# A DLRM tower with two cross layers: products of three fields summed over d on TensorE, and weights of both layers combined on the chip

## The chip, the cores and the metric

One core of one Trainium2 chip runs the whole kernel. The metric is the device time of one execution, in microseconds (us).

## The reference

Each of 1024 samples has 32 categorical fields, each an index into a table of its own; the rows fetched are vectors of 32 numbers d. Two cross layers follow, then a small tower. Everything is fp32.

```python
e = stack([tbl_f[ids[:, f]] for f in range(32)], axis=1)     # b, 32 fields, 32 d
x = e
for W in (W0, W1):                                           # W0: 1024 x 128, W1: 4096 x 128
    z = einsum('bhd,bmd->bhmd', e, x).reshape(b, 32 * prev, 32)
    x = einsum('bpd,pj->bjd', z, W)
    res.append(x)
z = sum(concatenate(res, axis=1), axis=-1)                   # sum over d: 256 numbers a sample
h = relu(concatenate([z, dense_ctx], axis=1) @ W_top1 + b_top1)
h = relu(h @ W_top2 + b_top2)
y = h @ W_top3
```

x1[j, d] is a weighted sum of products of two fields, and only its sum over d is used as an output; the second layer multiplies x1 by every field once more. So the output of the second layer is a weighted sum, over triples of fields, of the products of three fields summed over d.

## The kernel before

The work goes in 8 tiles of 128 samples. A tile has 4 units of 32 samples, which are gathered from the tables by POOL (32 indirect DMAs a tile, L272, 128 rows each), and 8 chunks of 16 samples, which are 512 columns (16 samples by 32 d).

Gathered rows lie in `emb`. SP stores them in DRAM (`scratch`, L204 to L213) and loads every chunk back as `fac` (L215 to L235): four reads with other strides put field pairs side by side on 128 partitions, so that three vector multiplications (L409, L417, L418) and one small one (L424) form all pairs of fields for 512 columns. Three quarters of the first layer's products are then split: ACT rounds them into `zh` (L285), DVE subtracts that from the exact value into `zl` (L429), and PE multiplies the high part by the high and the low half of the weights and the low part by the high half. This takes nine passes of the faster format fp32r (L476, L477, L480), one for the leftover pairs (L482), and one exact fp32 matmul of two instructions (L473). Their sum is x1 of the chunk, in `XO`.

Then, per chunk: ACT copies x1 out; DVE sums it over d (L441); PE transposes it (L489, 4 instructions) and multiplies it by the block-diagonal `eblk` (L514, 4 fp32 matmuls of two instructions each), which gives the sums over d of x1 times each field; ACT copies those into `G` (L314 to L321). Once a tile, 32 fp32 matmuls (L523, x2_products) multiply `G` by W1, and the tower runs (L534, L535, L544, L552: 22 fp32 matmuls of 128 columns).

The order is written by hand: in PE's loop (L589 to L605) chunk i's x1, the transposes of chunk i-1 and the products of chunk i-2 follow each other, and at fixed chunks of the next tile stand x2_products, hidden1, hidden2 and result. The other engines have loops of the same lags, and semaphores tie them. The last tile's end is last_tile (L555 to L583).

Of the kernel before, what the change touches and what calls it, by code (L numbers as in the profile page):

```python
# [6 lines left out]
F32R = mybir.dt.float32r  # L7
# [3 lines left out]
AX = mybir.AxisListType  # L11
# [16 lines left out]

def dlrm_cin_tower(nc, dense_t, ids, bases, table, w_top1, w_dense, vec_in, w_top2, w0_pairs, w0_rest, w1, scratch, out):
# [5 lines left out]
    F, D, J = N_FIELDS, DIM, P  # L35
# [3 lines left out]
    BANK = 512  # L39
    CHUNKS = P * D // BANK  # L40
    TOTAL = TILES * CHUNKS
    PAIRS = TOTAL // 2
    COLS = P * D
    BC = BANK // D
    GU = BC // NQ
    UNITS = 4
    PER = CHUNKS // UNITS
    UG = P // NQ // UNITS
    WIDTH = UG // NQ
    URUN = UG * D  # L50
    KT1 = 2
    N1, N2 = H1 // P, H2 // P
    WHOLE = 1
    SPLIT = SHIFTS - WHOLE
    RING = 6
    ZB = 3
    RAMP = 8
    RING16 = 4

    ctx = ExitStack()  # L60
    with ctx:
# [8 lines left out]

        ident = sb("ident", [P, P])
# [3 lines left out]
        w0f = sb("w0f", [P, SHIFTS, J])  # L75
        w0h = sb("w0h", [P, SPLIT, J], F32R)
        w0l = sb("w0l", [P, SPLIT, J], F32R)
        w16m = sb("w16m", [3 * F, 2, J], F32R)
        w1s = sb("w1s", [P, F, J])
        wt1 = sb("wt1", [P, KT1, H1])  # L80
# [7 lines left out]
        eblk = sb("eblk", [P, P // NQ, NQ, F])  # L88
        fac = [sb(f"fac{i}", [P, SHIFTS, BANK]) for i in range(RING)]
        b16 = [sb(f"b16{i}", [F, 2, BANK]) for i in range(RING16)]  # L90
        z = [sb(f"z{i}", [P, WHOLE, BANK]) for i in range(ZB)]
        zh = [sb(f"zh{i}", [P, SPLIT, BANK], F32R) for i in range(2)]
        zl = [sb(f"zl{i}", [P, SPLIT, BANK], F32R) for i in range(2)]
        z16 = sb("z16", [F, BANK])
        z16p = [sb(f"z16p{i}", [3 * F, BANK], F32R) for i in range(2)]
        x1 = [sb(f"x1{i}", [P, BC, D]) for i in range(3)]
        x1t = [sb(f"x1t{i}", [P, GU, P]) for i in range(2)]
        G = sb("G", [P, F, P])
        zf = sb("zf", [P, KT1, B])
# [4 lines left out]
        XO = [ps(f"XO{i}", [P, BANK]) for i in range(2)]  # L104
        U0 = ps("U0", [P, BANK])
        U1 = ps("U1", [P, BANK])
        ZS = ps("ZS", [P, SPLIT, BANK])
        WA = ps("WA", [P, BANK])
        M = WA[:, :].rearrange("p (a b) -> p a b", b=P)
# [5 lines left out]
        w1_loaded = sem("w1_loaded")  # L115
        tower_loaded = sem("tower_loaded")
        prep = sem("prep")
        eblk_zero = sem("eblk_zero")
        tower_zero = sem("tower_zero")
        wt3_made = sem("wt3_made")  # L120
        rows_made = sem("rows_made")
        gathered = [[sem(f"gathered{i}{j}") for j in range(UNITS)] for i in range(2)]
        stored = [sem(f"stored{j}") for j in range(UNITS)]
        et_made = sem("et_made")
        eblk_made = sem("eblk_made")
        loaded = [sem(f"loaded{i}") for i in range(RING)]
# [532 lines left out]
```

## Time and profile before

| what | us |
|---|---|
| median of 3 runs | 464.38 |
| lowest, highest | 462.21, 464.61 |
| profiled execution, own time | 463.55 |
| its span, first to last instruction | 461.7 |
| PE busy (matmul) | 407.0 |
| DVE busy | 355.7 |
| POOL busy | 310.7 |
| ACT busy | 293.5 |

The profiled execution's own time is 1.85 us over its span. Busy times are unions of instruction records on one engine. A matmul record's end lies after the start of the next one, so the pace of PE is read from start to start, or from a run of many divided by their count. An fp32 matmul is two instructions, a transpose or an fp32r matmul is one.

### The profile page before, as it was taken

To read this page: it belongs to the slowest core of one execution; us is meant where nothing else is said; L and a number is where in the kernel's file an instruction comes from. 1 tells how busy PE (TensorE), PEld (TensorE's weight loads), DVE (VectorE), ACT (ScalarE), POOL (GpSimd) and SP (SyncE) were. 2 spreads that over 40 slices of the span, in tenths; PEclk is the share of its full clock that TensorE was granted. 3 is DMA by queue.
4 is the path that set the end of the run, shared out by engine and by line. 5 is a ranking of instruction groups with operands and counts; after the bars stand their busy time and mean duration, and the time that the engine had idled before them with its cause. 6 is when DMAs were issued, how large, how long until landed. Compare 5 with 4: busy or idle time off the path is not lost.

```text
span 461.7 us, 7268 instructions
## 1 busy us (share of the span) xinstructions
PE 407.0 (88%) x2464; PEld 330.3 (72%) x2464; DVE 355.7 (77%) x399; ACT 293.5 (64%) x512; POOL 310.7 (67%) x262
## 2 busy tenths in 40 slices
PE   0014788889999999999999999999999999999987
PEld 0002456569877788868888888788888988798887
DVE  6024798997699888976989968997899689978700
ACT  1011577674677757864788588876788478847841
POOL 6777777887788787878787878788787777000000
PEclk9999999999999999999999999999999999999999
DMA  7368899775887668999899789888777659992000
GB/s 277 100 144 211 210 222 219 231 211 140 181 244 221 198 186 213 176 207 223 204 211 219 184 201 243 213 217 215 223 228 210 182 144 220 214 267 60 1 1 0
DMA packets 56659, 86.25 MB, mean 187 GB/s; under 512 B 10696, under 2 KB 21136, under 8 KB 56496
## 3 DMA queue, kind: packets, MB, share of 16 engines
q1 hardware_dynamic: 48432, 81.59, 62.4%
q0 software_dynamic: 8192, 4.21, 10.4%
q8 instruction: 20, 0.33, 0.4%
q14 instruction: 15, 0.12, 0.1%
HBM read 79.47 MB, written 6.30 MB: 186 GB/s over the span
## 4 chain that ended last, share of the span: by engine, by line
PE 54%; POOL 30%; issue 9%; DMA 4%; DVE 2%; ACT 1%; SPq 1%; POOLq 0%; DVEq 0%
POOL emb L272 30%; PE WA L523 9%; PE U L514 7%; PE XO L473 7%; PE XO L480 6%; PE XO L477 6%; PE XO L476 6%; PE U L489 4%; PE WA L544 2%; PE WA L534 2%; PE XO L482 2%; DMA fac<-scratch 2%; DMA emb<-in_table,rows 1%; PE WA L535 1%; PE WA L499 1%
## 5 line engine op out<-in xcount | busy, mean ns | idle before, releaser
L272 POOL DMA_INDIRECT emb<-in_table,rows x256 | 310.0, 1211 | 80.2 <-issue 77.7
L429 DVE TENSOR_TENSOR zl<-ZS,zh 128x1536 fp32r<-128x1536 f32 x64 | 112.1, 1752 | 34.5 <-ACT zh L279 34.4
L279 ACT ACTIVATE zh<-ZS 128x1536 fp32r<-128x1536 f32 x64 | 93.1, 1455 | 67.2 <-issue 39.3
L476 PE MATMUL XO<-zh,w0h 128*128 128x512 f32 x192 | 98.9, 515 | 2.8 <-ACT zh L279 2.8
L473 PE MATMUL XO<-z,w0f 128*128 128x512 f32 x128 | 67.4, 609 | 31.1 <-DVE z L409 31.1
L418 DVE TENSOR_TENSOR ZS<-fac 128x1024 f32<-128x1024 f32 x64 | 78.1, 1220 | 0.0
L477 PE MATMUL XO<-zh,w0l 128*128 128x512 f32 x192 | 76.9, 401 | 0.0
L409 DVE TENSOR_TENSOR z<-fac 128x512 f32<-128x512 f32 x64 | 43.8, 685 | 42.3 <-DMA fac<-scratch 41.9
L480 PE MATMUL XO<-zl,w0h 128*128 128x512 f32 x192 | 57.4, 407 | 13.2 <-DVE zl L429 12.7
L514 PE MATMUL U<-eblk,x1t 128*128 128x128 f32 x504 | 67.2, 276 | 0.0
L279 ACT ACTIVATE G<-U 128x512 f32<-128x512 f32 x63 | 38.0, 603 | 43.2 <-PE WA L523 40.7
L514 PEld LDWEIGHTS U<-eblk,x1t 128*128 128x128 f32 x504 | 61.2, 192 | 0.3
L476 PEld LDWEIGHTS XO<-zh,w0h 128*128 128x128 f32 x192 | 36.9, 192 | 31.3 <-ACT zh L279 13.6
L523 PE MATMUL WA<-G,w1s 128*128 128x128 f32 x512 | 58.5, 275 | 0.0
L523 PEld LDWEIGHTS WA<-G,w1s 128*128 128x128 f32 x512 | 57.8, 192 | 0.0
L480 PEld LDWEIGHTS XO<-zl,w0h 128*128 128x128 f32 x192 | 35.2, 190 | 27.6 <-DVE zl L429 20.1
L279 ACT ACTIVATE eblk<-WA 32x256 f32<-32x256 f32 x128 | 48.0, 375 | 6.5 <-PE WA L499 2.8
L477 PEld LDWEIGHTS XO<-zh,w0l 128*128 128x128 f32 x192 | 36.9, 192 | 18.2 <-issue 12.2
L441 DVE TENSOR_REDUCE zf<-x 128x16 f32<-128x512 f32 x64 | 43.2, 677 | 5.8 <-ACT x L279 4.9
L417 DVE TENSOR_TENSOR ZS<-fac 128x512 f32<-128x512 f32 x64 | 44.1, 690 | 1.1
L489 PE MATMUL U<-ident,x 128*128 128x128 f32 x256 | 38.7, 273 | 5.1 <-ACT x1t L279 5.1
L473 PEld LDWEIGHTS XO<-z,w0f 128*128 128x128 f32 x128 | 20.0, 196 | 31.3 <-issue 31.1
(76 smaller groups left out, 380.7 us busy)
## 6 DMA issues: line engine op xcount, KB each, us to landing
fac<-scratch SPq DMA_DIRECT2D x256, 256.0 KB
emb<-in_table,rows POOLq DMA_INDIRECT x256
scratch<-emb SPq DMA_DIRECT2D x32, 128.0 KB
b<-scratch SPq DMA_DIRECT2D x64, 64.0 KB, 6.1
w1s<-in_W SPq DMA_DIRECT2D x1, 2048.0 KB, 8.4
scratch<-emb SPq DMA_DIRECT2D x32, 64.0 KB
wt<-in_W_top SPq DMA_DIRECT2D x2, 512.0 KB, 9.4
z<-in_W_pairs SPq DMA_DIRECT2D x2, 256.0 KB, 2.8
```

The costliest lines, as they stand in the source:

```text
L272: eng.indirect_dma_start(emb[par][:, g, :], None, table, bass.IndirectOffsetOnAxis(rows[:, k, g:g + 1], 0))\
L279: return eng.activation(dst, src, ACT.Copy)
L417: eng.tensor_tensor(ZS[:, 0, :], f[:, 0, :], f[:, 3, :], ALU.mult).then_inc(zs_first, 1)
L418: eng.tensor_tensor(ZS[:, 1:, :], equal, fac[s][:, 2:4, :], ALU.mult).then_inc(zs_done, 1)
L429: eng.tensor_tensor(zl[i % 2][:, :, :], ZS[:, :, :], zh[i % 2][:, :, :].bitcast(F32), ALU.subtract)\
L473: eng.matmul(o, w0f[:, t, :], zb[:, t, :], start=(t == 0), stop=False)
L476: eng.matmul(o, w0h[:, t, :], zh[b][:, t, :], start=(WHOLE == 0 and t == 0), stop=False)
L477: eng.matmul(o, w0l[:, t, :], zh[b][:, t, :], start=False, stop=False)
L480: eng.matmul(o, w0h[:, t, :], zl[b][:, t, :], start=False, stop=False)
L489: t = eng.transpose(U0[:, P * u:P * u + P], flat[:, P * u:P * u + P], ident[:, :])
L514: m = eng.matmul(g_bank(i)[:, P * u:P * u + P], x1t[i % 2][:, u, :], eblk[:, at, :, :].rearrange("p v h -> p (v h)"), start=True, stop=True)
L523: m = eng.matmul(WA[:, 0:P], w1s[:, h, :], G[:, h, :], start=(h == 0), stop=(h == F - 1))
```

## The change

DRAM scratch, the loads from it, the split into high and low parts and x1 itself are gone. What takes their place:

- **Products.** Gathered units are transposed on PE (`ET`: partition = sample and d, column = group and field; a group is 4 samples, a unit 8 groups). ACT copies `ET` into the block-diagonal `eblk` of 33 columns a sample (32 fields and one of ones; 4 copies of 32 partitions) and once plainly into `eT`. DVE multiplies `ET` (PSUM) by `eT` (SBUF) in 11 instructions a unit (products, in three parts): all unordered pairs of the first 16 fields, all of the last 16.
- **Triples.** One slot is three groups (the third slot of a unit has two). For each group PE multiplies the transposed pairs (128 columns for `TA`, 128 for `TB`, 32 for `T3`) by `eblk` (132 columns): each result is a product of three fields summed over d. There are 96 slots, 24 matmuls a unit.
- **Copies.** ACT copies `TA` and `TB` into `TS` in three pieces each (side_copy), DVE copies `T3` in five (rest_copy). The bank `T3` is single, `TA` and `TB` are double.
- **Combined weights.** Before the loop PE multiplies W1 by W0 plus its transposed pair (w0_w1: 32 times 272 and 256 columns). In the first tile DVE adds what belongs to the same triple (weights, 12 portions, 70 additions and 4 copies). In slots 12 to 18 PE transposes the 56 blocks and ACT copies them to `C`.
- **Both outputs.** A tile is then 56 matmuls of 128 columns for the second layer (second) and 7 for the first (first), and the tower as before. Tile 0's stand in slots 19 to 26, those of tiles 1 to 6 in the slots of the tile after, tile 7's at the end.

The number of gathers, their size, the tower and the outputs stay. The diff, cut:

```diff
-            def load(k, n):
-                i = CHUNKS * k + n
-                at = scratch.offset + k * ROWS * COLS + BANK * n
-                if n % PER == 0:
-                    eng.wait_ge(stored[n // PER], STORES * (k + 1))
-                wait(eng, zs_done, i - RING + 1)
-                for a in range(2):
-                    eng.dma_start(fac[i % RING][:, a, :],
-                                  bass.AP(scratch.tensor, at + (4 - 4 * a) * COLS, [[COLS, F], [0, 4], [1, BANK]]))\
-                       .then_inc(loaded[i % RING], 16)
...
-            def products_split(i):
-
-                s = i % RING
-                f = fac[s][:, :, :]
-                wait(eng, zl_done, i)
-                equal = bass.AP(f.tensor, f.offset + BANK, [list(f.ap[0]), [0, 2], [1, BANK]])
-                eng.tensor_tensor(ZS[:, 0, :], f[:, 0, :], f[:, 3, :], ALU.mult).then_inc(zs_first, 1)
-                eng.tensor_tensor(ZS[:, 1:, :], equal, fac[s][:, 2:4, :], ALU.mult).then_inc(zs_done, 1)
...
-            def products(i):
-                zb, b, o = z[i % ZB], i % 2, XO[i % 2][:, :]
-                wait(eng, x1_kept, i - 1)
-                eng.wait_ge(z_done, i + 1)
-                for t in range(WHOLE):
-                    eng.matmul(o, w0f[:, t, :], zb[:, t, :], start=(t == 0), stop=False)
-                eng.wait_ge(zh_done, i + 1)
-                for t in range(SPLIT):
-                    eng.matmul(o, w0h[:, t, :], zh[b][:, t, :], start=(WHOLE == 0 and t == 0), stop=False)
-                    eng.matmul(o, w0l[:, t, :], zh[b][:, t, :], start=False, stop=False)
-                eng.wait_ge(zl_done, i + 1)
-                for t in range(SPLIT):
-                    eng.matmul(o, w0h[:, t, :], zl[b][:, t, :], start=False, stop=False)
-                eng.wait_ge(z16l_done, i // 2 + 1)
-                eng.matmul(o, w16m[:, i % 2, :], z16p[i // 2 % 2][:, :], start=False, stop=True).then_inc(x1_made, 1)
-
...
+            def w0_w1(h):
+
+                if h % (F // W1P) == 0:
+                    eng.wait_ge(w1_loaded[h // (F // W1P)], 16)
+                wait(eng, rt_kept, h - 1)
+                eng.matmul(TA[h % 2][:, 0:RTC], w1s[:, h, :], sym[:, 0:RTC], start=True, stop=True).then_inc(rt_made, 1)
+                p, x = divmod(h, 2)
+                if x == 0:
+                    wait(eng, rx_kept, p - 1)
+                m = eng.matmul(TB[p % 2][:, RAB * x:RAB * x + RAB], w1s[:, h, :], sym[:, RTC:], start=True, stop=True)
+                if x == 1:
+                    m.then_inc(rx_made, 1)
...
+            def full_adds(X, second, part):
+
+
+                Y = 1 - X
+                f, c = across(X)
+                if part == 0:
+                    dst = rt(HALF * Y, P * X + 64, [[RTC, HALF], [SUB, SUB], [1, SUB]])
+                    src = rx(HALF * X + SUB, 0, [[c, HALF], [f, SUB], [RAB, SUB]]) if second else \
+                        rx(HALF * X, SUB * f, [[c, HALF], [RAB, SUB], [f, SUB]])
+                    add(dst, dst, src, second_added if second else first_added)
+                    return
...
+            def products(u, part):
+
+                both = 2 * GROUPS
+                pairs, rest = zT[u % 2][:, :, :], z3[u % 2][:, :, :]
+
+                def apart(s):
+                    some = [[HALF, both], [SUB, 2], [1, SUB - s]]
+                    eng.tensor_tensor(view(pairs, off(s), [[P, both], [32, 2], [1, SUB - s]]), field(0, some), copied(s, some),
+                                      ALU.mult).then_inc(z_made, 1)
+
+                if part == 0:
+                    eng.wait_ge(eblk_made, (NQ + 1) * (u + 1))
+                    wait(eng, t3_made, TRIOS * (u - 1))
+                    eng.tensor_tensor(view(pairs, 64, [[P, both], [SUB, SUB], [1, SUB]]),
+                                      field(0, [[HALF, both], [1, SUB], [0, SUB]]),
+                                      copied(SUB, [[HALF, both], [0, SUB], [1, SUB]]), ALU.mult).then_inc(z_made, 1)
+                if part == 1:
+                    for s in range(1, 5):
+                        apart(s)
+                if part == 2:
+                    for s in range(5, SUB):
+                        apart(s)
+                    some = [[HALF, both], [SUB, 2], [1, 4]]
+                    eng.tensor_tensor(view(pairs, PAIRS, [[P, both], [32, 2], [1, 4]]), field(0, some), copied(0, some),
+                                      ALU.mult).then_inc(z_made, 1)
+                    some = [[F, GROUPS], [SUB, 4], [1, 4]]
+                    eng.tensor_tensor(view(rest, 0, [[THIRD, GROUPS], [4, 4], [1, 4]]), field(4, some), copied(4, some),
+                                      ALU.mult).then_inc(z_made, 1)
+                    eng.tensor_copy(view(rest, MORE, [[THIRD, GROUPS], [1, HALF]]), field(0, [[F, GROUPS], [1, HALF]]))\
+                       .then_inc(z_made, 1)
+
+            def rest_copy(t):
...
+                for q in range(NQ):
+                    eng.tensor_copy(view(ts[32 * q:32 * q + 32, :, :], P * REST + b0, [[4 * P, 2], [P, 4], [1, n]]),
+                                    view(T3[0:32, :], q, [[HALF + 1, 2], [4, 4], [C33, n]])).then_inc(t3_kept, 1)
+                eng.tensor_copy(ts[0:32, REST1, b0:b0 + n], view(T3[0:32, :], ONES, [[C33, n]])).then_inc(t3_kept, 1)
...
+            def side_copy(X, t, made, kept):
...
+                copy(view(ts[:, :, :], P * FULL[X] + b0, [[P, HALF + 1], [1, n]]),
+                     view(bank[:, :], full, [[1, HALF + 1], [C33, n]])).then_inc(kept, 1)
+                for e in range(2):
+                    at = (HALF + 1 if X else 0) + SUB * e
+                    copy(view(ts[64 * e:64 * e + 64, :, :], P * OWNS[X] + b0, [[P, SUB], [1, n]]),
+                         view(bank[0:64, :], at, [[1, SUB], [C33, n]])).then_inc(kept, 1)
+
+            def c_copy(q):
...
+            def triples(t):
...
+                    eng.wait_ge(rt_kept, F)
+                    eng.wait_ge(rx_kept, F // 2)
+                wait(eng, ta_kept, 3 * (t - 1))
+                pairs, rest = zT[u % 2], z3[u % 2]
+                for bank, z, cols, made in ((TA[t % 2], pairs, slice(0, P), ta_made), (TB[t % 2], pairs, slice(P, 2 * P), tb_made),
+                                            (T3[0:THIRD, :], rest, slice(0, THIRD), t3_made)):
+                    if made is tb_made:
+                        wait(eng, tb_kept, 3 * (t - 1))
+                    if made is t3_made:
+                        wait(eng, t3_kept, 5 * t)
+                    for x, g in enumerate(trio(r)):
+                        at = NQ * C33 * x
+                        m = eng.matmul(bank[:, at:at + NQ * C33], z[:, g, cols],
+                                       eblk[u % 2][:, g, :, :].rearrange("p v c -> p (v c)"), start=True, stop=True)
+                    m.then_inc(made, 1)
+
+            def second(k, pieces):
+                if pieces[0] == 0:
+                    eng.wait_ge(ta_kept, 3 * SLOTS_TILE * (k + 1))
+                    eng.wait_ge(tb_kept, 3 * SLOTS_TILE * (k + 1))
+                    eng.wait_ge(t3_kept, 5 * SLOTS_TILE * (k + 1))
+                    eng.wait_ge(c_kept, CB)
+                    wait(eng, y2_kept, k)
+                for kt in pieces:
+                    m = eng.matmul(WA[:, 0:P], C[:, kt, :], TS[k % 2][:, slot_of(kt), :], start=(kt == 0), stop=(kt == KT - 1))
+                if pieces[-1] == KT - 1:
+                    m.then_inc(y2_made, 1)
...
+        def y2_range(t):
+
+
+            k, j = divmod(t, SLOTS_TILE)
+            if k == 1:
+                return (0, range(14 * (j - 7), 14 * (j - 7) + 14)) if 7 <= j < 11 else None
+            if k > 1 and j < KT // Y2_PER:
+                return k - 1, range(Y2_PER * j, Y2_PER * j + Y2_PER)
+            return None
```

A chunk of 16 samples on PE before, with the waits on semaphores in brackets (`XO` is x1, `U` the banks of the transposes and of the products, `ZS` holds the products to be split):

```order
L473 MATMUL XO<-z,w0f 128x512 [waits z_done,x1_kept]
L476 MATMUL XO<-zh,w0h 128x512 [waits zh_done]
L477 MATMUL XO<-zh,w0l 128x512
L476 MATMUL XO<-zh,w0h 128x512
L477 MATMUL XO<-zh,w0l 128x512
L476 MATMUL XO<-zh,w0h 128x512
L477 MATMUL XO<-zh,w0l 128x512
L480 MATMUL XO<-zl,w0h 128x512 [waits zl_done]
L480 MATMUL XO<-zl,w0h 128x512 x2
L482 MATMUL XO<-z16p,w16m 128x512 [waits z16l_done]
L489 MATMUL U<-ident,x 128x128 [waits xt_kept,x1_kept]
L489 MATMUL U<-ident,x 128x128 x3
L514 MATMUL U<-eblk,x1t 128x128 [waits eblk_made,g_kept,xt_kept]
L514 MATMUL U<-eblk,x1t 128x128 x3
```

One unit of 32 samples in the steady part of the change on PE, which begins with the transposes of the unit after it (`T` is `T3`, `RX` holds the combined weights):

```order
L640 MATMUL ET<-ident,emb 128x128 [waits z_made,gathered03]
L640 MATMUL ET<-ident,emb 128x128
L661 MATMUL TA<-eblk,zT 128x132 [waits ta_kept,z_made]
L661 MATMUL TA<-eblk,zT 128x132 x2
L661 MATMUL TB<-eblk,zT 128x132 [waits tb_kept]
L661 MATMUL TB<-eblk,zT 128x132 x2
L661 MATMUL T<-eblk,z 32x132 [waits t3_kept]
L661 MATMUL T<-eblk,z 32x132 x2
L673 MATMUL WA<-TS,RX 128x128 x7
L661 MATMUL TA<-eblk,zT 128x132 [waits ta_kept]
L661 MATMUL TA<-eblk,zT 128x132 x2
L661 MATMUL TB<-eblk,zT 128x132 [waits tb_kept]
```

The first matmul of a unit waits for z_made, the eleven products of that unit, which DVE makes while PE works at the unit before it. Every `T` group waits for t3_kept, DVE's copies of the slot before.

DVE in the first tile of the change, from the first product of unit 1 on:

```order
L534 TENSOR_TENSOR zT<-ET,eT 128x16x64 [waits eblk_made]
L564 COPY TS<-T 32x8x12 [waits t3_made]
L564 COPY TS<-T 32x8x12 x3
L566 COPY TS<-T 32x12
L401 TENSOR_TENSOR RT<-RT,RX 128x16x64 [waits rx_kept,rt_kept]
L528 TENSOR_TENSOR zT<-ET,eT 128x16x2x7
L528 TENSOR_TENSOR zT<-ET,eT 128x16x2x6
L528 TENSOR_TENSOR zT<-ET,eT 128x16x2x5
L528 TENSOR_TENSOR zT<-ET,eT 128x16x2x4
L564 COPY TS<-T 32x8x12 [waits t3_made]
L564 COPY TS<-T 32x8x12 x3
L566 COPY TS<-T 32x12
```

Between the copies of `T` and the next products stands an addition to the weights. In later tiles the rows of L401 are missing, and the others come in the same order. Of before, one chunk on DVE:

```order
L435 TENSOR_TENSOR z16p<-z,z16p 32x512 [waits z16h_done]
L417 TENSOR_TENSOR ZS<-fac 128x512 [waits zl_done]
L418 TENSOR_TENSOR ZS<-fac 128x1024
L441 TENSOR_REDUCE zf<-x 128x2x8 [waits x1_kept]
L409 TENSOR_TENSOR z<-fac 128x512 [waits x1_made,loaded4]
L429 TENSOR_TENSOR zl<-ZS,zh 128x1536 [waits x1_made,zh_done]
```

The six rows became, for a unit, eleven products and fifteen copies of at most 1024 columns, tied to PE at both ends.

## Rows read from the trace of the kernel before

**Rows 1.** The page: engines, granted clock in 40 slices, chain by engine

```profile
PE 407.0 (88%) x2464; PEld 330.3 (72%) x2464; DVE 355.7 (77%) x399; ACT 293.5 (64%) x512; POOL 310.7 (67%) x262
...
PEclk9999999999999999999999999999999999999999
...
PE 54%; POOL 30%; issue 9%; DMA 4%; DVE 2%; ACT 1%; SPq 1%; POOLq 0%; DVEq 0%
```

**Rows 2.** Windows: busy us (instructions) of PE, PEld, DVE, ACT, POOL; clock, DMA, GB/s

```profile
31.00:41.00 10.00, 4.97 (x8) 2.32 (x8) 2.58 (x4) 2.59 (x3) 7.56 (x9) 1.00 0.62 161
51.00:61.00 10.00, 7.02 (x32) 4.31 (x31) 6.70 (x8) 7.37 (x12) 7.87 (x8) 1.00 0.90 232
200.00:440.00 240.00, 238.68 (x1494) 199.31 (x1493) 207.71 (x231) 173.92 (x305) 153.89 (x125) 1.00 0.77 192
```

**Rows 3.** Chain in order of time: start us, us, what, instructions

```profile
357.99 7.15 PE WA L523 x64
...
392.88 0.86 PE XO L473 x2
396.49 0.89 PE U L514 x8
...
407.26 7.15 PE WA L523 x64
```

**Rows 4.** Timeline of PE, 43 to 50 us: start us, us, instruction

```profile
43.20 1.65 PE L480 MATMUL XO<-zl,w0h 128*128 128x512 f32 x3 [5.88 <-DVE zl L429]
...
48.22 0.63 PE L476 MATMUL XO<-zh,w0h 128*128 128x512 f32 x1
48.65 0.58 PE L477 MATMUL XO<-zh,w0l 128*128 128x512 f32 x1
49.06 0.40 PE L476 MATMUL XO<-zh,w0h 128*128 128x512 f32 x1
49.29 0.39 PE L477 MATMUL XO<-zh,w0l 128*128 128x512 f32 x1
```

**Rows 5.** Timeline of DVE and POOL, 385.5 to 389.5 us

```profile
385.41 1.76 DVE L429 TENSOR_TENSOR zl<-ZS,zh 128x1536 fp32r<-128x1536 f32 x1 [0.25 <-ACT zh L279]
...
386.28 0.94 POOL L272 DMA_INDIRECT emb<-in_table,rows  x1 [0.30 <-issue]
...
387.20 0.70 DVE L417 TENSOR_TENSOR ZS<-fac 128x512 f32<-128x512 f32 x1
...
387.81 1.23 DVE L418 TENSOR_TENSOR ZS<-fac 128x1024 f32<-128x1024 f32 x1
...
388.95 0.67 DVE L424 TENSOR_TENSOR z<-b 32x512 f32<-32x512 f32 x1
389.01 1.43 POOL L272 DMA_INDIRECT emb<-in_table,rows  x1 [0.30 <-issue]
```

**Rows 6.** Groups: busy us, mean ns of one, idle before and releasers

```profile
L473 PE MATMUL XO<-z,w0f 128*128 128x512 f32 x128 | 67.4, 609 | 31.1 <-DVE z L409 31.1
...
L279 ACT ACTIVATE eblk<-WA 32x256 f32<-32x256 f32 x128 | 48.0, 375 | 6.5 <-PE WA L499 2.8
...
L489 PE MATMUL U<-ident,x 128*128 128x128 f32 x256 | 38.7, 273 | 5.1 <-ACT x1t L279 5.1
L279 ACT ACTIVATE x1t<-U 128x512 f32<-128x512 f32 x64 | 38.2, 598 | 0.3 <-PE U L489 0.3
...
L279 ACT ACTIVATE G<-U 128x512 f32<-128x512 f32 x63 | 38.0, 603 | 43.2 <-PE WA L523 40.7 <-PE U L514 2.3
...
L279 ACT ACTIVATE zf<-WA 128x128 f32<-128x128 f32 x8 | 2.2, 273 | 8.3 <-PE WA L523 8.3
...
L461 DVE TENSOR_SCALAR h<-XO,vec 128x128 f32<-128x128 f32 x2 | 0.7, 351 | 13.0 <-PE XO L570 13.0
```

**Rows 7.** Timeline of DVE, the first 10 us

```profile
6.40 3.47 DVE L390 MEMSET eblk<- 128x4096 f32 x1 [0.80 <-issue]
```

**Rows 8.** Timeline, the end of the span

```profile
455.56 0.28 ACT L279 ACTIVATE zf<-WA 128x128 f32<-128x128 f32 x1 [8.34 <-PE WA L523]
```

More of the change, by code:

```diff
@@ new lines, in own_adds @@
+            def own_adds(e, second):
+                f, c = (SUB, 1) if e == 0 else (1, SUB)
+                for s in range(1, SUB) if second else range(0, SUB):
+                    n = SUB - s if s else 4
+                    col = 32 * e + (off(s) if s else PAIRS)
+                    dst = own(0, 1 - e, col, [[XO, 2], [P, SUB], [1, n]])
+                    one = dst if second else rt(SUB * (1 - e), col, [[XS, 2], [RTC, SUB], [1, n]])
+                    h, other = (s, 0) if second else (0, s)
+                    two = rt(SUB * e + h, 64 + f * other, [[XS, 2], [c, SUB], [RTC + f, n]])
+                    add(dst, one, two, second_added if second else first_added)
@@ new lines, in _ @@
+            eng.wait_ge(w0_loaded, 16 * 2)
+            eng.tensor_tensor(sym[:, :], sym[:, :], raw, ALU.add).then_inc(sym_made, 1)
+            eng.wait_ge(zeroed, 5)
+            for i in range(2):
+                for v in range(NQ):
+                    eng.memset(eblk[i][DIM * v:DIM * v + DIM, :, v, ONES], 1.0).then_inc(ones_set, 1)
+            eng.wait_ge(y1_loaded, 16 * 2)
+            eng.tensor_tensor(y1w[:, :, :], y1w[:, :, :], raw_y1, ALU.add).then_inc(y1w_made, 1)
+            for part in range(3):
+                products(0, part)
@@ L457, in _ @@
+            for t in range(TOTAL):
+                u, r = divmod(t, TRIOS)
+                if u + 1 < ALL:
+                    products(u + 1, r)
+                rest_copy(t)
+                if t < SLOTS_TILE:
+                    weights(t)
             eng.wait_ge(tower_loaded, 16 * 5)
@@ L524, in x2_products @@
-                m.then_inc(x2_made, 1)
+                for x, slot in enumerate(Y1_SLOTS):
+                    m = eng.matmul(M[:, 0, :], y1w[:, x, :], TS[k % 2][:, slot, :], start=(x == 0), stop=(x == Y1T - 1))
+                m.then_inc(y1_made, 1)
             def hidden1(k):
-                rows = slice(P * k, P * k + P)
-                eng.wait_ge(x2_kept, k + 1)
-                eng.wait_ge(summed, CHUNKS * (k + 1))
-                wait(eng, eblk_made, min(NQ * (UNITS * (k + 1) + 2), NQ * UNITS * TILES))
+                eng.wait_ge(y1_kept, k + 1)
@@ new lines, in _ @@
+            for h in range(F):
+                w0_w1(h)
+                if h == 24:
+                    emb_transposes(0)
+            for t in range(TOTAL):
+                u, r = divmod(t, TRIOS)
+                if r == 0 and u + 1 < ALL:
+                    emb_transposes(u + 1)
+                triples(t)
+                if SLOTS_TILE <= t < SLOTS_TILE + CB // 2:
+                    for q in range(2):
+                        weights(2 * (t - SLOTS_TILE) + q)
+                if y2_range(t) is not None:
+                    second(*y2_range(t))
+                if tile_at(t, Y1_AT) is not None:
+                    first(tile_at(t, Y1_AT))
+                if tile_at(t, L1_AT) is not None:
+                    hidden1(tile_at(t, L1_AT))
+                if tile_at(t, L2_AT) is not None:
+                    hidden2(tile_at(t, L2_AT))
+                if tile_at(t, Y_AT) is not None:
+                    result(tile_at(t, Y_AT))
```

692 lines of the change are left out of this document (351 added, 341 removed).

## The prediction

> **What bounds the kernel now.** I read the page first. PE is busy for 407.0 us of 461.7, DVE and ACT for 355.7 and 293.5 [rows 1]. The chain of waits names POOL for 30%, which could mislead: in the windows PE is busy for 238.68 of the 240 us from 200 to 440 [rows 2], so from there on nothing but PE counts, and POOL is only what the chain meets when followed back through the first tiles. From one run of x2_products to the next the chain shows 49.27 us, a tile [rows 3]. The same view gives PE's prices: 7.15 us for 32 fp32 matmuls of 128 columns, so 0.2235 each; 0.89 for four; 0.86 for one of 512 columns. The timeline of PE shows 0.23 us from one fp32r matmul of 512 columns to the next [rows 4]. A tile is 8 chunks of 0.86 + 10 x 0.23 + 4 transposes of 0.15 (38.7 us over 256) [rows 6] + 0.89, that is 8 x 4.65 = 37.2, then 7.15, the tower's 22 x 0.2235 = 4.9, and 8 transposes of units, 1.2: 50.5 us, against 49.27 measured. PE runs with no gap worth naming, and every change to its work in the steady tiles is worth its face value.
>
> **What goes.** Per tile the x1 matmuls, both kinds of chunk transposes and products, and x2_products: 8 x 4.65 + 7.15 = 44.4 us of PE. The scratch DMAs, the four large products, the split and the sum over d go too. In the steady part they lie beside PE and are worth nothing, but the first gather, store and load keep PE waiting for 31.1 us [rows 6].
>
> **What comes, in order of time.**
>
> *Setup.* DVE's memsets before the large one stay, and end at 5.6 us [rows 7]. The new ones (2 x 1056, 2 x 128 and 512 numbers, 2880) cost 2880 / 4096 x 3.47 = 2.4 us, with the gap of 0.8 us that stands before the large one now [rows 7]; the sum of the transposed W0 is 528 columns, 0.6. PE starts at 9.7 us. Its 32 steps of 528 columns cost 0.86 x 528 / 512 = 0.89 each, 28.4 us. The clock adds to that: in the timeline fp32r matmuls follow each other every 0.43 us until 49.06 and every 0.23 after that, though the page grants 1.0 in every slice [rows 1, 4]: levels of 1.2 and 2.4 GHz. The engine had been busy without a long gap since 43.20, 5.9 us, so a cold start costs half of that, 2.9 us. Copies of unit 0 on ACT within this phase 0.6, unit transposes 0.3, the last weight copies 0.8. The first slot starts at **42.7 us**.
>
> *The chain through a unit.* The first triple of a unit waits for eleven products, and those go through three engines. Transposes 0.4; ACT's four eblk copies 0.39 each and eT 0.35 (between 273 ns at 128 and 598 at 512 columns) [rows 6], with the hand-overs 2.5 us in all. DVE: a number costs 1.04 ns (0.61 us from L417 to L418 with 512 columns, 1.14 from L418 to L424 with 1024 [rows 5]). What an instruction costs beyond it is the disputed size. Starts of SBUF operations give 0.06 us; the nearest row, L429, reads PSUM and SBUF as the products do, 1.76 us for 1536 columns, so 0.16; two operations from PSUM in 351 ns each for 128 columns give 0.21 [rows 5, 6]. I take 0.15 for products and 0.18 for copies, since these change their 32 partitions as the eblk copies do. Eleven products with 2304 columns: 2.40 + 1.65 = 4.05. Copies of a slot of 12 samples (396 columns, 5 instructions): 0.41 + 0.90 = 1.31, two of them in the chain, 2.6. With the last hand-over 9.25 us; 7.1 with 0.06 everywhere, 10.2 with 0.21.
>
> The Trainium skill (VectorE: DVE Perf Modes, on the TRN2 errata) gives a vector operation from PSUM 120 cycles and one from SBUF 58, by my estimate 0.125 and 0.06 us. By that the chain would be some 0.5 us shorter and the total 3 us lower; the trace agrees on SBUF.
>
> *Tile 0.* PE has only 24 triples (132 columns, 0.2304 each, 5.53) and two transposes, 5.8 us a unit, so the chain sets the pace, and the weight additions stand in it. They are 11.4 thousand columns, 11.9 us, and 74 instructions of 0.06, 4.5: 16.4 us, of which the portions after each unit's first two slots, 11.6, are in the chain; the others run while ACT copies, and 0.3 shows. 4 x 9.25 + 11.9 = 48.9. PE would be busy for 46% of this, between the 50% at which it still ran at half pace from 31 to 41 us and nothing measured lower; from 51 to 61, at 70%, it ran at full pace [rows 2]. At half pace the triples of a slot take 4.1 us for 2.1, DVE's copies start after them and not after the products, and the same sum makes a unit 0.95 longer, 3.8 in the tile. I take half, 1.9. **50.8**.
>
> *Tile 1.* Two units of weight transposes: PE 8.6, the chain 9.3, 18.6 in all. Then the units with 14 second-layer matmuls a slot: 5.83 + 1.2 + 28 x 0.2235 = 13.3, and 5.83 + 35 x 0.2235 = 13.65, both PE's. **45.6**.
>
> *Tiles 3 to 7.* PE: 96 x 0.2304 = 22.1, 8 transposes 1.2, and 56 + 7 + 22 matmuls 19.0: 42.3 us, 10.6 a unit over a chain of 9.25. I add 0.1. **212.0**. The price of 132 columns has no row; it lies between 0.2235 and 0.25, and 768 of them at 0.25 would add 15 us. I scale with the columns, as 0.2235 for 128 and 0.86 for 512 do within 4%. *Tile 2* also has tile 0's tower, 4.9: **47.2**.
>
> *ACT and POOL, at nothing.* ACT has six copies a slot of 204 and 96 columns, 0.35 and 0.26 us at most, 5 us a unit, with eblk 2.0 and a quarter of a tile's tower, 0.8: under 8, hidden by PE's 10.6. If PE were quicker by 2.5 us a unit, it would set the pace. POOL starts a gather every 1.25 us (0.94 + 0.30), and is stretched to 1.43 where DVE runs operations on two SBUF tensors (L424, L418); beside L429, which reads PSUM, it is not [rows 5]. Only the weight additions are of that kind afterwards: 5 for the start + 256 x 1.25 + at most 16.4 = 341 us, and the last unit is needed at about 375. DMA queues: SP's stores and loads vanish, nothing is queued behind the new w1 pieces that is needed early.
>
> *The end.* After the last triple: T3's copies 1.3, 7 + 48 + 4 + 8 + 4 matmuls of 0.2235, 15.9, then from the copy of y2 to the end as now, 461.7 - 455.56 - 0.3 for the part already counted = 5.8 [rows 8]. **23.0**.
>
> Sum: 42.7 + 50.8 + 45.6 + 47.2 + 212.0 + 23.0 = 421.3 us of span; with 1.85 us around it 423.2, against the profiled execution's 463.55 (whose runs have a median of 464.38). I forecast **423 us**.
>
> **Rivals.**
>
> *The chain is the bound in every tile.* Its margin is 1.35 us a unit, and it has 21 DVE instructions. At 11 us (0.08 us more for each): tile 0 +7, tile 1 +3.5, tiles 2 to 7 +8, so 442. For: single buffers `ET` and `T3`. Against: L429's row. At about 11.8 us the gain is gone.
>
> *Scattered operands cost DVE two cycles a number: slower.* The change reads and writes in runs of 1 to 8 numbers, and T3 33 apart; before, every large operation on DVE ran over 512 in a row. Then the chain's 3096 columns cost 3.2 us more, 12.45: tile 0 +12.8, tile 1 +6.3, tile 2 +2.6, the others 20 x 1.85 = +37, additions in the chain +8: 490 us. From 0.4 of a cycle more it shows in every tile, and from about three quarters the change loses. Against: ACT's copy into `G` reads PSUM 32 numbers apart, in 603 ns, and `x1t` the same size in a row in 598 [rows 6]. That is ACT; no row shows DVE.
>
> [...]
>
> *The gather becomes the bound.* Its average now is 1.51 us: 310.7 busy over 256, and 0.30 between two [rows 1, 5]. At that pace the last unit comes at 5 + 387 = 392; its chain, triples, the end and what is around the span are 9.3 + 6 + 23 + 1.85: 432 us. Against: the stretching belongs to DVE operations that go.
>
> *PE falls back to half pace in tile 0 and stays there into tile 1*: +1.9, and two units of 17 us of half-pace work until it recovers, +3: 428. The Trainium skill (TensorE: Matmul & The Clock Gate, what's actually happening) has the engine drop to half rate after idling; rows show only that it began so.
>
> That the change doesn't do what it says is excluded by the order of instructions above.
>
> **How the numbers follow.** Forecast with the clock cases 0.76, chain at 10.5 to 11.5 us 0.12, gather 0.03, scattered operands 0.05, something unnamed 0.04, half of it a loss. Low end: chain 7.1 (-8.6 in tile 0, -1.4 in tile 1), no clock loss (-1.9): 411. High end: chain 11 and the clock, 442 + 4 = 446. A measurement tells 0.5%, 2.3 us, from no change. Faster 0.93, same 0.01, slower 0.06.
>
> **What would show it.** First `triples` matmul at about 43 us. Tiles 3 to 7 of 42.4 us each between the runs of y1w matmuls, PE busy over 97%. In tile 0 PE waits for DVE's products, most of all. Products of 224 columns near 0.38 us, T3 copies near 0.3. Gathers at 1.25 us from tile 1 on. Wrong if PE has waits on z or T3 in tiles 3 to 7, if the copies of 96 columns take over 0.45 us, or if the triples are over 0.24 us apart.

## The result, and the profile after

The changed kernel takes **443.06 us** (median of 4 runs, 442.48 to 444.81) beside 464.45 us for the kernel before in the same comparison. The ratio is 0.9556, 95% interval 0.9517 to 0.9596: 4.4% faster. The forecast was 423, its range 411 to 446. So the sign held and the size didn't: 21.4 us of the 41 forecast came. The time lies inside the range, but by luck: the upper end stood for a longer chain through DVE and for the clock, and neither makes most of the miss that follows.

The profiled execution took 442.48 us with a span of 440.6, 19.3 over the 421.3 that the terms of the prediction make. In the page of the kernel after, the engines' busy time, the granted clock in 40 slices and the chain by engine answer to [rows 1]:

```profile
PE 408.4 (93%) x3144; PEld 367.8 (83%) x3144; DVE 236.5 (54%) x926; ACT 233.4 (53%) x870; POOL 260.8 (59%) x262
...
PEclk9999788669999999999999999999999999999999
...
PE 85%; DVE 10%; ACT 2%; issue 1%; DMA 0%; SPq 0%
```

PE is the bound as forecast, but it is busy for as long as before, 408.4 us, although a steady tile was to take 42.3 us of it for 49.27. The granted clock is lower from the fifth slice to the ninth (44 to 99 us), in tile 0 and at the start of tile 1. Two windows of the kernel after (columns as in [rows 2]), tile 0 nearly whole, and the end of tile 2 with most of tile 3, a steady tile:

```profile
43.00:94.00 51.00, 32.78 (x193) 27.10 (x193) 47.33 (x172) 22.42 (x90) 42.49 (x28) 0.77 0.05 10
187.00:229.00 42.00, 42.00 (x344) 37.94 (x343) 23.30 (x95) 24.01 (x96) 31.81 (x34) 1.00 0.08 14
```

In tile 0 DVE is busy for 47.33 of 51 us. In the steady tile PE never idles by its records. Every tile starts with the transposes of a unit (`ET`), in tile 0 those of unit 1; in the timeline of PE after these are the starts of tiles 0, 1, 2, 3 and 7, and of the end:

```profile
40.43 0.38 PE L640 MATMUL ET<-ident,emb 128*128 128x128 f32 x2
...
92.53 0.66 PE L640 MATMUL ET<-ident,emb 128*128 128x128 f32 x2 [1.76 <-DVE z L549]
...
141.84 0.38 PE L640 MATMUL ET<-ident,emb 128*128 128x128 f32 x2
...
191.99 0.38 PE L640 MATMUL ET<-ident,emb 128*128 128x128 f32 x2
...
372.94 0.38 PE L640 MATMUL ET<-ident,emb 128*128 128x128 f32 x2
...
418.91 1.80 PE L685 MATMUL M<-TS,y1w 128*128 128x128 f32 x14 [0.79 <-DVE TS L566]
```

| term of the sum | forecast | after | difference |
|---|---|---|---|
| setup | 42.7 | 40.43 | -2.3 |
| tile 0 | 50.8 | 52.10 | +1.3 |
| tile 1 | 45.6 | 49.31 | +3.7 |
| tile 2 | 47.2 | 50.15 | +3.0 |
| tiles 3 to 7 | 212.0 | 226.2 | +14.2 |
| the end | 23.0 | 22.4 | -0.6 |
| span | 421.3 | 440.6 | +19.3 |

(Tiles 3 to 6 take 372.94 - 191.99 = 180.95, 45.24 each; tile 7 is taken as the same, so it ends at 418.2.) The miss lies where nothing waits. The timeline of PE shows it, one slot of a steady tile:

```profile
237.45 0.84 PE L661 MATMUL TA<-eblk,zT 128*128 128x132 f32 x6
238.13 0.84 PE L661 MATMUL TB<-eblk,zT 128*128 128x132 f32 x6
238.89 0.86 PE L661 MATMUL T<-eblk,z 128*32 128x132 f32 x6
239.69 1.83 PE L673 MATMUL WA<-TS,RX 128*128 128x128 f32 x14
241.35 0.73 PE L661 MATMUL TA<-eblk,zT 128*128 128x132 f32 x5
```

Six instructions (three fp32 matmuls) from `TA` to `TB` take 0.68 us, 0.113 each. The six of `TB`, with the way to `T`, take 0.76, and the six of `T` 0.80. The 14 of L673 take 1.66, 0.09 over 14 x 0.112. Nine triples take 2.24 us on the way from the first `TA` to L673, 0.249 each, and more than 0.24 was one of the prediction's signs of being wrong. `T` is the group whose stationary operand, by the shape in its row, has 128 rows by 32 columns instead of 128 by 128. The timeline of the weight loads, same place:

```profile
238.01 0.75 PEld L661 LDWEIGHTS TB<-eblk,zT 128*128 128x128 f32 x6
238.89 0.59 PEld L661 LDWEIGHTS T<-eblk,z 128*32 128x32 f32 x6
239.69 1.64 PEld L673 LDWEIGHTS WA<-TS,RX 128*128 128x128 f32 x14 [0.20 <-issue]
```

The first load for `TB` starts at 238.01, 0.12 before its matmul. The first for `T` starts at 238.89, with its matmul, and that of L673 at 239.69, also with its own, after 0.20 us of idle. Where the shape changes, the next load isn't made ahead.

The Trainium skill (TensorEngine Tiling (Array Packing), in the section on key properties) says that changing the tiling mode drains the engine. Among its available configurations it lists 128x64 and 128x32 beside 128x128. The rows agree as far as they go: the next load starts only with its matmul, and the start is 0.09 us late.

**Theory A**, to be tested: every excursion from 128 stationary columns to 32 and back costs about 0.3 us. There are 96 of them, one a slot, and the 12 of tile 0 are hidden, since PE waits there anyway. **Its rival B**: nothing is lost by the shape, and PE is slow there because of something else in the slot (a wait that the profile doesn't show, a dearer 132 columns, traffic with the copies). For tile 0: the chain through DVE, the clock, or scattered operands.

### The profile page after: what moved, and what is told of

It reads as the page before. It is cut to its first block, busy times and chain, and to the rows that moved or that the text cites. A ratio compares the mean times of both kernels' runs of the same rounds, so it can differ in the third digit from the quotient of the medians.

```text
span 440.6 us, 8640 instructions
## 1 busy us (share of the span) xinstructions
PE 408.4 (93%) x3144; PEld 367.8 (83%) x3144; DVE 236.5 (54%) x926; ACT 233.4 (53%) x870; POOL 260.8 (59%) x262
## 4 chain that ended last, share of the span: by engine, by line
PE 85%; DVE 10%; ACT 2%; issue 1%; DMA 0%; SPq 0%
PE WA L673 25%; PE T L661 14%; PE TA L661 12%; PE TB L661 12%; PE TA L609 3%; PE M L685 3%; PE M L704 3%; PE M L695 3%; PE TB L613 3%; DVE RT L401 3%; DVE TS L564 2%; PE ET L640 2%; PE M L696 1%; ACT eblk L283 1%; DVE zT L528 1%
## 5 line engine op out<-in xcount | busy, mean ns | idle before, releaser
L564 DVE COPY TS<-T 32x96 f32<-32x96 f32 (+1 forms) x384 | 90.7, 236 | 75.8 <-PE T L661 66.9
L673 PE MATMUL WA<-TS,RX 128*128 128x128 f32 x896 | 114.2, 281 | 0.0
L673 PEld LDWEIGHTS WA<-TS,RX 128*128 128x128 f32 x896 | 104.1, 191 | 10.7 <-issue 10.5
L283 ACT ACTIVATE TS<-TA 64x96 f32<-64x96 f32 (+3 forms) x288 | 64.3, 260 | 61.7 <-PE TA L661 59.3
L661 PE MATMUL T<-eblk,z 128*32 128x132 f32 x512 | 78.2, 287 | 10.0 <-DVE TS L566 10.0
L661 PE MATMUL TA<-eblk,zT 128*128 128x132 f32 x512 | 77.2, 285 | 0.6 <-ACT RX L283 0.6
L661 PE MATMUL TB<-eblk,zT 128*128 128x132 f32 x512 | 76.1, 283 | 0.0
L661 PEld LDWEIGHTS T<-eblk,z 128*32 128x32 f32 x512 | 49.7, 112 | 24.4 <-DVE TS L566 11.4
L661 PEld LDWEIGHTS TA<-eblk,zT 128*128 128x128 f32 x512 | 67.7, 197 | 2.6 <-issue 2.6
L661 PEld LDWEIGHTS TB<-eblk,zT 128*128 128x128 f32 x512 | 67.8, 197 | 0.0
L283 ACT ACTIVATE TS<-TB 64x96 f32<-64x96 f32 (+3 forms) x288 | 64.8, 259 | 4.6
```

What stands on the lines that cost most here:

```text
L283: return eng.activation(dst, src, ACT.Copy)
L564: eng.tensor_copy(view(ts[32 * q:32 * q + 32, :, :], P * REST + b0, [[4 * P, 2], [P, 4], [1, n]]), view(T3[0:32, :], q, [[HALF + 1, 2], [4 ...
L661: m = eng.matmul(bank[:, at:at + NQ * C33], z[:, g, cols], eblk[u % 2][:, g, :, :].rearrange("p v c -> p (v c)"), start=True, stop=True)
L673: m = eng.matmul(WA[:, 0:P], C[:, kt, :], TS[k % 2][:, slot_of(kt), :], start=(kt == 0), stop=(kt == KT - 1))
```

## Experiments

Measured beside the experiments, the kernel before had medians of 464.41 us (1, 2, 4 and 6) and 464.44 us (3, 5, 7 and 8), so their times can be set beside 443.06. Ratios are to the kernel before.

**1. The stationary operand of T3 padded with zeros to 128 columns.** The result in the 32 partitions used is the same, and PE multiplies the same number of moving columns. The only thing added is two memsets on DVE before the loop.

```diff
+Z3W = 128
-        z3 = [sb(f"z3{i}", [P, GROUPS, THIRD]) for i in range(2)]
+        z3 = [sb(f"z3{i}", [P, GROUPS, Z3W]) for i in range(2)]
+                eng.memset(z3[i][:, :, THIRD:], 0.0).then_inc(zeroed, 1)
-                                            (T3[0:THIRD, :], rest, slice(0, THIRD), t3_made)):
+                                            (T3[0:Z3W, :], rest, slice(0, Z3W), t3_made)):
```

> The stationary operand of the third triple group is padded from 32 to 128 columns with zeros, nothing else. Theory (going from 128 stationary columns to 32 and back stops PE): the gaps of 0.206, 0.137, 0.206 and 0.213 us around the T3 matmuls shrink to 0.112, a slot loses 0.31 us, a steady tile falls from 45.2 to 41.5 us, and 84 to 96 slots give 26 to 30 us: 413 to 417 us. Rival (the wait for DVE's copies of T3 is what costs): nothing changes, 443 us. A third outcome: the DVE chain of a unit appears as a new bound near 10.4 us a unit and keeps part of it, 418 to 428 us.

Measured: **418.2 us**, 24.9 less than the change, ratio 0.8997 (0.8949 to 0.9044). Timeline of PE of the padded kernel, the same slot:

```profile
228.13 0.84 PE L665 MATMUL TA<-eblk,zT 128*128 128x132 f32 x6
228.81 0.84 PE L665 MATMUL TB<-eblk,zT 128*128 128x132 f32 x6
229.49 0.84 PE L665 MATMUL T<-eblk,z 128*128 128x132 f32 x6
230.16 1.72 PE L677 MATMUL WA<-TS,RX 128*128 128x128 f32 x14
231.72 0.73 PE L665 MATMUL TA<-eblk,zT 128*128 128x132 f32 x5
```

Now it is 0.68, 0.68, 0.67 and 1.56: 3.59 us a slot for 3.90. And the load is ahead again:

```profile
228.70 0.75 PEld L665 LDWEIGHTS TB<-eblk,zT 128*128 128x128 f32 x6
229.38 0.75 PEld L665 LDWEIGHTS T<-eblk,z 128*128 128x128 f32 x6
230.05 0.86 PEld L677 LDWEIGHTS WA<-TS,RX 128*128 128x128 f32 x7
```

A steady tile went from 45.24 to 41.46 us (tile starts at 186.46 and 227.92), 3.78 for 12 slots, 0.315 a slot. Loading four times the columns cost nothing. B falls: only the shape was changed, and PE waits for nothing in tiles 3 to 7 here either, so the third outcome, the chain as a new bound, isn't seen. The time is 1.2 us over the 417 of the theory: in the profiled executions tiles 1 to 7 and the end give 25.7 us, and the setup takes 1.5 more than in the change, for a reason that is its own (see *Setup* below).

**2. Two excursions a slot.** The last group of `TB` is issued between the groups of `T3`, so the engine leaves 128 columns twice; no work is added.

```diff
-                    m.then_inc(made, 1)
+                    last = len(trio(r)) - 1
+                    for x in range(last + (made is ta_made)):
+                        m = group(x)
...
+                    if made is t3_made:
+                        tb_last(last).then_inc(tb_made, 1)
+                        group(last).then_inc(made, 1)
```

> The same matmuls, but in every slot the last TB matmul stands between the T3 matmuls, so that PE goes to 32 stationary columns and back twice a slot. Theory: 0.31 us more in each of the 84 slots in which PE is the bound, 26 us, 469 us. Rival (T3's bank or copies cost, not the way in and out): the same number of matmuls and waits, 443 us, at most 3 more for T3 being asked for 0.2 us earlier.

Measured: **469.04 us** (8 runs, 467.81 to 470.42), 26.0 more than the change, ratio 1.0098 (1.0069 to 1.0126). Timeline of PE:

```profile
249.83 0.61 PE L661 MATMUL TB<-eblk,zT 128*128 128x132 f32 x4
250.37 0.64 PE L661 MATMUL T<-eblk,z 128*32 128x132 f32 x4
250.94 0.49 PE L661 MATMUL TB<-eblk,zT 128*128 128x132 f32 x2
251.36 0.41 PE L661 MATMUL T<-eblk,z 128*32 128x132 f32 x2
251.70 1.83 PE L682 MATMUL WA<-TS,RX 128*128 128x128 f32 x14
```

From the first `TB` row shown to L682 12 instructions and two more switches take 1.87 us; in the change they take 1.56 (238.13 to 239.69). A steady tile takes 49.02 us for 45.24, again 3.78 more, without a wait of PE in it. Doubling the suspected cost doubled it, and that alone put the kernel 1% above the kernel before.

**3. Padded to 64 columns.** Experiment 1 with `Z3W = 64`: is it 32 that costs, or anything but 128?

> The stationary operand of the third group is padded to 64 columns in place of 128. If every change of the number of stationary columns stops PE: about as the change itself, 442 to 444 us, steady tile 45.2 us. If only 32 columns do: 418 us, steady tile 41.5. If the stop grows with how much of the array is left out: between, about 430 us.

Measured: **445.6 us**, ratio 0.9601 (0.955 to 0.9651), 2.5 us more than with 32 columns and nearest to the first outcome. Timeline of PE:

```profile
240.35 0.84 PE L665 MATMUL TB<-eblk,zT 128*128 128x132 f32 x6
241.12 0.89 PE L665 MATMUL T<-eblk,z 128*64 128x132 f32 x6
241.94 1.83 PE L677 MATMUL WA<-TS,RX 128*128 128x128 f32 x14
```

0.77 and 0.82, for 0.76 and 0.80 with 32 columns: 64 columns cost as much and a little more. A steady tile takes 45.56 us, 0.34 a slot over the padded kernel's.

**4. Extra matmuls in tile 0, for the clock.** The timeline of PE after at the second unit of tile 0:

```profile
52.52 0.66 PE L640 MATMUL ET<-ident,emb 128*128 128x128 f32 x2 [1.87 <-DVE z L549]
52.97 1.53 PE L661 MATMUL TA<-eblk,zT 128*128 128x132 f32 x6
54.29 1.53 PE L661 MATMUL TB<-eblk,zT 128*128 128x132 f32 x6
...
57.77 0.84 PE L661 MATMUL TB<-eblk,zT 128*128 128x132 f32 x6
```

From `TA` to `TB` 1.32 us pass, about twice 0.68: the 1.2 GHz level, after a wait of 1.87 us. By 57.77 the pace is full again. The edit puts matmuls whose result nobody reads where PE waits (8 a slot, 16 instructions):

```diff
+                if t < SLOTS_TILE:
+                    for _ in range(8):
+                        eng.matmul(WA[:, 0:P], ident[:, :], ident[:, :], start=True, stop=True)
```

> Eight fp32 matmuls of 128 columns on the identity follow the triples in each of the first 12 slots (1.8 us a slot at full pace), into a bank that nobody reads then. If the half pace of PE at the start of each unit lengthens tile 0: tile 0 falls from 52.1 to about 49 us and the first unit of tile 1 from 11.5 to 9.7, 438 to 440 us. If DVE alone sets tile 0: 443 us. If the extra matmuls stand in the way themselves: 445 to 450 us.

Measured: **439.06 us**, 4.0 less, ratio 0.9447 (0.9396 to 0.9498). The window from 60 to 80 us in the change and here:

```profile
60.00:80.00 20.00, 10.29 (x61) 8.35 (x60) 18.34 (x70) 7.05 (x29) 16.95 (x11) 0.76 0.05 8
```

```profile
60.00:80.00 20.00, 19.15 (x156) 17.07 (x155) 19.30 (x73) 8.13 (x35) 16.95 (x11) 1.00 0.06 9
```

With the extra matmuls PE is busy for 19.15 of 20 us at a granted clock of 1.00 (10.29 and 0.76 without), and DVE is busy for 19.30 of 20 us. Tile 0 gained only 1.9 us (52.1 to 50.2, where 3 were expected), since DVE sets its pace at either clock, by its busy time; the first unit of tile 1 gained 2.3 (11.47 to 9.13).

**5. Padding and extra matmuls together.**

> 128 columns for the third group and the eight extra matmuls in each slot of tile 0 together. If the two effects are independent: 418.2 - 4.0 = 414 us. If the padding had already done the extra matmuls' work for the pace of PE in tile 0: 418 us.

Measured: **414.69 us**, ratio 0.8945 (0.8898 to 0.8991), 3.5 under experiment 1. The two gains add up, nearly.

**6. The weight additions left out.** This kernel leaves out the 34 additions of `full_adds` (7,936 columns a partition; the text of the expectation counts 30), so its combined weights lack those terms.

```diff
             def full_adds(X, second, part):
+                return
-        FIRST_ADDS, SECOND_ADDS = 36, 32
+        FIRST_ADDS, SECOND_ADDS = 18, 16
```

> The 30 additions of RX to RT are left out (7936 of 11400 columns of the weight additions), so the second layer's weights are incomplete. Theory (the additions stand in tile 0's chain at what they take, 11 us of them after first and second slots): tile 0 falls from 52.1 to about 41 us, 432 us. Rival (tile 0 is PE's, at half pace): PE's 24 triples at half pace are 11.3 us a unit, tile 0 stays at 47 or more, 438 us.

Measured: **428.98 us**, 14.1 less, ratio 0.9233 (0.9186 to 0.9281). Tile 0 fell from 52.1 to 38.6 us, 9.2 to 10.1 a unit, in the profiled execution (426.83 us). The groups of the change give the 34 additions, 16.1 us:

```profile
L401 DVE TENSOR_TENSOR RT<-RT,RX 128x128 f32<-128x128 f32 (+7 forms) x34 | 16.1, 528 | 0.0
```

Tile 0 is 13.5 us shorter, but not by the additions alone: PE's granted clock in it is 0.96 for 0.79 as well, and experiment 4 gives the clock 1.9 us of tile 0. So by estimate 11.6 to 13.5 of the 16.1 us stood on the path: most of what DVE does there does. The first unit of tile 1 is 2.3 us shorter too (9.15), as in experiment 4.

**7. The additions with operands in a row.** `RX` is read 1 number apart where most additions read it 16, 256, 257 or 272 apart, with the same sizes and writes; the sums are therefore of other numbers.

```diff
-                    src = rx(HALF * X + SUB, 0, [[c, HALF], [f, SUB], [RAB, SUB]]) if second else \
-                        rx(HALF * X, SUB * f, [[c, HALF], [RAB, SUB], [f, SUB]])
+                    src = rx(HALF * X, 0, [[RAB, HALF], [SUB, SUB], [1, SUB]])
-                    src = rx(HALF * X + h, f * other, [[c, HALF], [SUB * RAB + SUB * f, 2], [RAB + f, n]])
+                    src = rx(HALF * X, other, [[RAB, HALF], [32, 2], [1, n]])
```

> The 30 additions into RT read RX with step 1 in place of steps of 16 and 256 numbers, same sizes (so the weights are wrong sums). If the step costs (1024 columns in 1.20 us with step 1, 1.89 with 16 or 256): the RT additions fall from 16.1 to about 11 us of DVE, 3 to 4 us of it in tile 0's chain, 439 to 440 us. If POOL's gathers, which overlap them, are what stretches them: they stay at 1.9 us and the time at 443.

Measured: **439.05 us**, 4.0 less, ratio 0.9451 (0.9394 to 0.9507). Timeline of DVE in the change, the first two large additions; the second reads `RX` in runs of 8 numbers as it is:

```profile
45.57 1.89 DVE L401 TENSOR_TENSOR RT<-RT,RX 128x1024 f32<-128x1024 f32 x1
47.39 1.06 DVE L528 TENSOR_TENSOR zT<-ET,eT 128x224 f32<-128x224 f32 x4
48.38 1.07 DVE L564 COPY TS<-T 32x96 f32<-32x96 f32 x4
49.48 0.16 DVE L566 COPY TS<-T 32x12 f32<-32x12 f32 x1
49.57 1.20 DVE L401 TENSOR_TENSOR RT<-RT,RX 128x1024 f32<-128x1024 f32 x1
...
52.30 0.94 DVE L564 COPY TS<-T 32x64 f32<-32x64 f32 x4
53.28 0.15 DVE L566 COPY TS<-T 32x8 f32<-32x8 f32 x1
```

The same two in this experiment:

```profile
46.73 1.20 DVE L401 TENSOR_TENSOR RT<-RT,RX 128x1024 f32<-128x1024 f32 x1
...
50.04 1.20 DVE L401 TENSOR_TENSOR RT<-RT,RX 128x1024 f32<-128x1024 f32 x1
```

The first fell from 1.89 to 1.20 us for 1024 numbers, and tile 0 to 48.4 (41.59 to 90.0). POOL's gathers beside these two still take 2.01 and 2.37 us, so it isn't they that stretch the additions.

**8. Both repairs, and tile 0 split between two engines.** ACT is busy for 22.42 of 51 us in tile 0, DVE for 47.33. So in the first 12 slots the copies of `T3` go to ACT; with Z3W = 128, and 4 extra matmuls a slot (8 in experiment 5; the granted clock of tile 0 is 1.00 in both). The first lines are ACT's loop, the last DVE's.

```diff
+                if t < SLOTS_TILE:
+                    rest_copy(t)
...
-                rest_copy(t)
+                else:
+                    rest_copy(t)
```

> 128 columns, four extra matmuls a slot, and in tile 0 the five copies of T3 of each slot go from DVE to ACT. DVE was busy for 47 of tile 0's 51 us and ACT for 22. If tile 0 is DVE's sum: a unit falls from 13 us to the longer of DVE's 8.6 and ACT's 10.5, about 42 us for the tile, 407 us. If the chain through ACT's eblk copies becomes the bound, since they now stand behind T3's copies: 11.5 to 12 us a unit, 411 us.

Measured: **406.03 us** (404.25 to 407.07), ratio 0.8741 (0.8689 to 0.8792), the best of all: 37 us under the change, 58 under the kernel before. Tile 0 takes 39.7 us (40.80 to 80.47) for the 50.2 of experiment 5. Window of this kernel from 41 to 92 us, tile 0 and the first unit of tile 1:

```profile
41.00:92.00 51.00, 45.01 (x373) 42.63 (x372) 42.31 (x142) 44.77 (x183) 42.46 (x29) 1.00 0.06 11
```

Every engine is busy for 42 to 45 of 51 us. What is late next is the gather, once, in its timeline of PE:

```profile
91.39 0.60 PE L660 MATMUL ET<-ident,emb 128*128 128x128 f32 x2 [1.94 <-DMA emb<-in_table,rows]
91.79 1.52 PE L681 MATMUL TA<-eblk,zT 128*128 128x132 f32 x6
93.11 1.52 PE L681 MATMUL TB<-eblk,zT 128*128 128x132 f32 x6
```

PE waits 1.94 us for rows, and falls back to half pace (1.32 from `TA` to `TB` again), and tile 1 takes 47.96 us for the 45.03 of experiment 5. So of the 10.5 us of tile 0 7.4 reached the end by the two profiled executions, and 8.7 by the medians; the profiled one of this kernel is the longest of its four (407.07 us).

## Why the prediction was right and wrong

**The step that failed** is "*Tiles 3 to 7.* PE: 96 x 0.2304 = 22.1, 8 transposes 1.2, and 56 + 7 + 22 matmuls 19.0: 42.3 us". It takes a matmul's price from its moving columns alone. This term makes 14.2 of the 19.3 us that were missing. I asked whether 132 columns scale, which they do better than I took (0.225 a matmul, and a transpose 0.109 for the 0.15 from a group's mean): without switches a tile is 41.46 us, 0.8 under the 42.3. What I did not ask is that a third of these matmuls have 32 stationary columns, where every matmul of the kernel before has 128. The order of the change showed `32x132` between rows of `128x132`; no row of before could price it, and so it needed bounds from both sides, which it didn't get. Measured: 0.31 us a slot, 3.78 a tile, about 26 us over the seven tiles that PE binds, which is the price of the switches that the sum lacked. Experiment 1 took it away (-24.9 us), experiment 2 doubled it (+26.0).

**Tile 1** (45.6, measured 49.3) **and tile 2** (47.2, 50.15) missed by the same term; tile 1 also by up to 2.3 us of clock. Padded, tile 1 takes 46.05, and with the extra matmuls too (experiment 5) 45.03.

**Setup** (42.7, 40.43): steps of 0.89 held. PE began at 9.30 for 9.7. The cold start cost 1.6 us for 2.9, but this differs from run to run: in the change the first steps take 1.89 and 1.46 us and the others 0.89, in experiment 1 they take 1.89, 1.76, 1.76 and 1.20, which is 3.0 us over four of 0.89. That alone makes the setup of experiment 1 1.5 us longer (41.91), so the 2.9 were not wrong. Unit 0's transposes and copies cost 1.1 us for 0.9. The wait for the last weight copies (0.8) lies behind this boundary: PE waits 0.6 us for them in tile 0, and the first triple starts at 41.37.

**Tile 0** (50.8, 52.1) came close, with errors that cancel. Products cost 0.07 us beyond their columns, not 0.15 (the timeline under experiment 7 has four, of 224, 192, 160 and 128 columns, in 0.99 us, from 47.39 to 48.38), 3.5 us less in 44 products; the starts in [rows 5] themselves give 0.08 (0.61 less 0.53) for operations from SBUF, where the prediction read 0.06. The estimate of a chain "some 0.5 us shorter" comes to 0.8 by its own counts, 0.025 for each of 11 products and 0.055 for each of 10 copies. A unit without the large additions is 38.6 / 4 = 9.65 us, with the small ones still in it; the 9.25 taken was near, if anything high. The weight additions (68 and 4 copies in the trace, not 70 and 4) were to cost 16.4 us of DVE and took 24 (16.1 + 3.0 + 2.7 and 2.2 in smaller groups): the large ones read SBUF at strides, and experiment 7 took their 16.1 us to 11.4.

**The rivals.** *The chain is the bound in every tile*: false; PE has no wait for `z` or `T3` in tiles 3 to 7, and 18.2 of the 18.8 us of them lie between 40 and 93 us, in the waits of the kernel after (us in all, times, longest):

```profile
PE T L661 <- DVE TS L566: 10.0, 7, 2.5
...
PE ET L640 <- DVE z L549: 8.8, 4, 2.9
```

*Scattered operands*: right for one case out of two, and not for the copies of `T3`. Reads from SBUF 16 numbers apart cost 0.67 ns more each, worth 4.0 us here. The Trainium skill (SBUF — State Buffer, in the section on the DMA port swizzle, the note on cachelines) says that each access in SBUF that crosses to a new line of 16 bytes pays a penalty; 1.89 us for 1.20 agrees. Reads from PSUM 33 apart cost nothing more: four copies of 96 columns take 1.10 us (48.38 to 49.48), 0.275 each, and four of 64 take 0.98 (52.30 to 53.28). The difference is 0.12 us for 128 numbers, 0.94 ns each, where a number in a row costs 1.04. *The gather*: not in the change; it is what comes next once tile 0 is quick. *The clock*: true, in tile 0 and the first unit of tile 1; priced at 1.9 (inside the forecast) and 3, it is worth 1.9 and 2.3 in the profiled executions, 4.0 in all by the medians of experiment 4.

In tiles 3 to 7 PE waits for neither ACT nor a gather, as forecast. The end took 22.4 us for 23.0.

## What to carry to other kernels

List the shape of every stationary operand in the order in which PE meets them, not only the moving columns: a small block between full ones cost a stop on both sides here, and zero padding to the common shape was free, since the padded rows of the result aren't read. Where a new shape has no row in the old trace, that absence is itself a term, and needs a bound each way. In a stage that one vector engine bounds, sum the busy time of DVE and ACT and split the work between them before repairing the clock: the split gave 8.7 us here, the clock 4.0, and 3.5 in the padded kernel.

## What the runs showed of the hardware that was not expected

- From one matmul to the next with another number of stationary columns (128 to 32, 128 to 64, and back) 0.206 us pass where 0.113 pass otherwise, and the second instruction after each switch is late too: 0.31 us for a way out and back. The load of the stationary operand, else some 0.11 us ahead of its matmul, isn't ahead there. L482 in the kernel before has a stationary operand of 96 rows and 128 columns and shows no such gap (0.23 us on both sides, as between its neighbours). No matmul here has fewer rows than that.
- An addition on DVE of 1024 numbers takes 1.89 to 1.92 us when one of its operands is read from SBUF 16 or 256 apart, and 1.20 when it is read in a row.
- In tile 0 waits of PE of 1.8 to 3.0 us at a unit's start come with the 1.2 GHz level for the matmuls after them, and with 48 extra instructions a unit (experiment 4) the granted clock stayed at 1.00.
- Beside weight additions, which have two SBUF operands, 12 gathers took 1.85 to 3.11 us each. Nearly all others took 0.94 to 0.96, as one pair in the timeline of POOL after shows:

```profile
48.60 0.94 POOL L276 DMA_INDIRECT emb<-in_table,rows  x1 [0.30 <-issue]
49.85 2.35 POOL L276 DMA_INDIRECT emb<-in_table,rows  x1 [0.30 <-issue]
```
